# Node tiles on ScalarE's queue, the last panel's own units in its middle, passage steps by engine, the final scaling on two engines

## The chip, the cores and the metric

The kernel runs on one core of one Trainium2 chip. The metric is the device time of one execution in microseconds (us), as the median of several runs.

## The reference

`adj` is an 8192 x 8192 float32 matrix A, `x` is 8192 x 128. Everything is float32. Cut to what matters:

```python
# layer 0
Ap = a * A;  Ap[i, i] += 1 - a;  deg = Ap.sum(axis=1)
x = layernorm(x + relu((Ap @ x) / deg[:, None] @ W.T + b))
# layer 1
xt  = logmap0(x)                                     # row scale by artanh(norm)/norm
par = A   * sigmoid((xt @ wp[:d])[:, None] + (xt @ wp[d:])[None, :] + bp)
chi = A.T * sigmoid((xt @ wc[:d])[:, None] + (xt @ wc[d:])[None, :] + bc)
x = layernorm(x + proj(expmap0(par @ xt + chi @ xt)))
```

## The kernel before, in words

A is cut into blocks of 1024 x 1024, so there are 8 panels of rows. Every load of A is one DMA of 1 MiB (two tiles of 128 rows) and goes into one of 10 buffers, the ring: entries 0 to 6 from the start, 7 to 9 after layer 0. SyncE (SP) issues these loads in the order of the list LOADS, each when its entry is free.

**Layer 0** is a loop over 256 pairs (32 for each panel). TensorE multiplies a pair with two node tiles of x (L1108), and VectorE adds it to the sums for the degrees (L884, L888). The node tiles stand in xA. They come in 16 groups of four DMAs of 64 KiB (L498), and SP issues a group ahead of every second load of the first panel. TensorE waits at pair q for group q // 2. ScalarE's queue begins with nine small DMAs of constants, then loads a panel of x transposed. VectorE waits for the constants at pair 2, before it adds that pair.

After each panel comes its **passage**: some twenty steps on four engines (POOL folds the degree sums, PE sums them and applies W, VectorE and ScalarE normalise and take the log map, PE turns the result and makes the two score vectors). Each step has a tick (T_DEG, T_INV, ... T_COPY), the place in the loop at which every engine that takes part issues it. For the last panel the ticks run beside layer 1: tick t is issued ahead of unit LATE0 + 2t, on every engine alike (LATE0 is 154, the first unit after layer 0).

**Layer 1** has 512 units, one for each pair of panel p and tile jt of 128 rows. A unit is: two sigmoids on ScalarE (L720 chi, L737 par), a product with A's tile on POOL (L537) and one on VectorE (L986), their sum on VectorE (L995), and two matmuls of 512 columns on TensorE, which sum over jt (L1180). In the trace each of these stands as two records. Some units, the list APART, leave out the sum and use two more matmuls instead (L1186). 154 units run in layer 0's loop, the rest after it, panel by panel. Two units share a load of A and one of its transpose. The eight **own units** of a panel, those on the diagonal block, need only A: TensorE turns the tile itself (L1196, turn_own), and for that it waits for all four loads of the diagonal block, whose entries come free after the eighth turn. Own units stand last in each of panels 3 to 7. Units of panel 7 are numbers 448 to 511.

The par scores of a unit stand in a PSUM slot. There are two slots in turn until SLOT_THREE (unit LATE0 + 48), three from there, because the passage uses the other one (E). A fourth chi buffer is used from MORE (unit LATE0 + 30), and APART begins eight units after it.

**Finals.** After the last unit of a panel its sum is taken out (L760), squared (L771), reduced to norms (L1205, then a root, L776), turned (L1215), scaled and added to the residual (L1014), and normalised (L1022 to L793), in steps among the next panel's units. Panel 7's final has no units beside it. Its last steps are the eight pieces of the scaling on ScalarE (L793) and one store of 512 KiB (L486).

Of the kernel before, what the change touches and what calls it, by code (L numbers as in the profile page):

```python
# [11 lines left out]
P = 128  # L12
# [36 lines left out]
T_OWN = 27  # L49

def early_groups():
# [8 lines left out]
def plan():  # L61
# [18 lines left out]
    for p, tiles in order:  # L80
        if len(tiles) == UPP:
            own = range(p * TPP, (p + 1) * TPP)
            tiles = [jt for jt in tiles if jt not in own] + list(own)
        groups.append((p, tiles, NPAN - 1))
        units += [(len(groups) - 1, p, jt) for jt in tiles]
# [54 lines left out]

SLOT_TWO, SLOT_THREE = LATE0, LATE0 + 48

# [112 lines left out]

MORE = LATE0 + 30

# [20 lines left out]
def adj_resnorm_kernel(nc, x_g, xT, g_blk, a_blk, WT, b_row, alpha, w_par, b_par, w_chi, b_chi, out):  # L278
    with ExitStack() as ctx:
# [147 lines left out]
        bias_ready = sem("bias_ready")  # L427
        o_ready = sem("o_ready")
        out_done = sem("out_done")

# [22 lines left out]
        def _(sp):  # L453
# [35 lines left out]
            for kind, j, e, before, _ in LOADS:  # L489
                if kind == "pair":  # L490
                    r, q = divmod(j, PPP)
                    if r == 0 and q % 2 == 0:
                        G = q // 2
                        src = x_g[G].rearrange("(a t) (c s d) -> s a c t d", t=2, s=2, d=D)
                        for h in range(2):
                            for c in range(2):
                                at = G * GC + c * 2 * D
                                sp.dma_start(xA[h * P // 2:(h + 1) * P // 2, at:at + 2 * D]  # L498
                                             .rearrange("a (t d) -> a t d", t=2), src[h, :, c]).then_inc(x_in[G], 16)
                    src = g_blk[q // 4, r, (q % 4) * 2 * P:(q % 4 + 1) * 2 * P, :]  # L500
# [14 lines left out]
            store(NPAN - 2)  # L515
            store(NPAN - 1)
            sp.wait_ge(out_done, 16 * NPAN)

# [94 lines left out]
        def _(act):  # L613
# [174 lines left out]
            def final_normalise(k, i):  # L788
# [4 lines left out]
                ins = act.activation(t, t, ACT.Identity, bias=s_mb[:, j:j + 1], scale=s_rs[:, j:j + 1])  # L793
                if i == TPP - 1:
                    ins.then_inc(o_ready, 1)

            def final(k, step):
# [12 lines left out]
                if k == NPAN - 2:  # L810
                    if step == L_ROOT:
                        final_deviation(k)
                    if L_NORM <= step < L_NORM + TPP:
                        final_normalise(k, step - L_NORM)

            for dst, src in (
                (alph[:, :], alpha.rearrange("(a d) -> a d", a=1).to_broadcast([P, 1])),
# [8 lines left out]
                act.dma_start(dst, src).then_inc(const_in, 16)  # L826
            act.wait_ge(ident_ready, 4)
            load_xT(0)
            scale_xT(0)
# [10 lines left out]
            for n in range(N_EARLY, UNITS):  # L840
                if (n - LATE0) % 2 == 0:
                    passage(NPAN - 1, (n - LATE0) // 2)
                for k, (_, b) in enumerate(FINALS):
# [8 lines left out]
                sigmoids(n)  # L852
            k = NPAN - 1
            evacuate(k)
            square(k)
# [3 lines left out]
            final_deviation(k)  # L859
            for i in range(TPP):  # L860
                final_normalise(k, i)

        @block.vector
        def _(dve):
# [211 lines left out]
            for n in range(N_EARLY, UNITS):  # L1076
                if (n - LATE0) % 2 == 0:
                    passage(NPAN - 1, (n - LATE0) // 2)
                for k, (_, b) in enumerate(FINALS):
                    final(k, n - b)  # L1080
                if n == N_EARLY and PAIRS - 1 in UNIT_AT:
                    key(n - 1)
                first_product(n)
                key(n)
# [6 lines left out]
            variances(k)  # L1091
            final_inverse(k)

        @block.tensor
        def _(pe):
# [135 lines left out]
            for n in range(N_EARLY, UNITS):  # L1231
                if (n - LATE0) % 2 == 0:
                    passage(NPAN - 1, (n - LATE0) // 2)
                for k, (_, b) in enumerate(FINALS):
# [39 lines left out]
```

## Time and profile before

| | us |
|---|---|
| median of three runs (2233.01 to 2239.25) | 2234.77 |
| the profiled execution | 2237.35 |
| its span | 2235.5 |
| TensorE busy | 2039.8 |
| VectorE busy | 1935.9 |
| POOL busy | 1334.1 |
| ScalarE busy | 1326.9 |

The mean granted clock of TensorE is 0.976. Numbers below are from the profiled execution, in us from the start of its span. Layer 0 ends at about 1266, the last load of A is there at 2190.9, and the last matmul of layer 1 ends at 2215.3.

### The profile page before, as it was taken

What the parts mean: (1) busy time and instruction counts of PE and PEld (TensorE: products, weight loads), DVE (VectorE), ACT (ScalarE), POOL (GpSimd) and SP (SyncE); (2) the same over time, 40 slices, a digit from 0 to 9 for tenths busy, and PEclk for the clock granted to TensorE, in tenths of its full rate; (3) what the DMA queues carried; (4) which work ended last, traced back from release to release, by engine and by line L of the source; (5) the groups of instructions that cost most, each with busy time, mean ns of one, the idle gap of its engine ahead of it and who ended that gap; (6) DMA issues with size and microseconds to landing.
All of it is one profiled execution on the core that took longest, in us unless ns stands there. A gap on an engine that the chain in (4) does not pass through costs nothing. (4 is left out here: it accounts for less than half of the span.)

```text
span 2235.5 us, 18654 instructions
## 1 busy us (share of the span) xinstructions
PE 2039.8 (91%) x5240; PEld 919.1 (41%) x5240; DVE 1935.9 (87%) x1854; ACT 1326.9 (59%) x1512; POOL 1334.1 (60%) x607
## 2 busy tenths in 40 slices
PE   8999999999999999999999976998888889889886
PEld 3344444444444434444444432343344334334334
DVE  4676878988989988998998988898998998989996
ACT  0011324454454454453453587889888989999996
POOL 0000305435455555643543676999998998999995
PEclk9999999999999999999999988999999999999998
DMA  9998989899889988888888998999999999998992
GB/s 313 333 343 300 387 299 365 361 366 381 361 347 403 405 344 358 347 357 338 369 356 316 421 421 317 384 363 421 421 393 403 421 420 376 421 421 347 421 421 97
DMA packets 129207, 818.29 MB, mean 366 GB/s; under 512 B 14912, under 2 KB 27456, under 8 KB 33360
## 3 DMA queue, kind: packets, MB, share of 16 engines
q1 hardware_dynamic: 122304, 796.97, 89.1%
q10 hardware_dynamic: 6800, 20.13, 2.5%
q8 instruction: 43, 0.70, 0.1%
q14 instruction: 60, 0.49, 0.1%
HBM read 808.59 MB, written 8.45 MB: 365 GB/s over the span
## 5 line engine op out<-in xcount | busy, mean ns | idle before, releaser
L537 POOL TENSOR_TENSOR chi<-chi,ring 128x1024 f32<-128x1024 f32 x323 | 826.9, 2573 | 662.7 <-ACT chi L720 603.5
L1180 PE MATMUL ps<-keys,xtA 128*128 128x512 f32 x2048 | 986.4, 615 | 135.4 <-DVE keys L995 106.1
L1108 PE MATMUL ps<-ring,xA 128*128 128x512 f32 x2048 | 922.5, 600 | 37.9 <-DMA ring<-in_g_blk 33.6
L737 ACT ACTIVATE ps<-scores,prcr 128x1024 f32<-128x1024 f32 x472 | 521.9, 1106 | 389.5 <-DVE keys L995 379.2
L1180 PEld LDWEIGHTS ps<-keys,xtA 128*128 128x128 f32 x2048 | 382.3, 195 | 668.1 <-issue 629.0
L888 DVE TENSOR_TENSOR dsum<-dsum,ring 128x2048 f32<-128x2048 f32 x240 | 593.2, 2472 | 44.7 <-DMA ring<-in_g_blk 37.4
L1108 PEld LDWEIGHTS ps<-ring,xA 128*128 128x128 f32 x2048 | 386.5, 192 | 533.3 <-issue 468.8
L995 DVE TENSOR_TENSOR keys<-ps,chi 128x1024 f32<-128x1024 f32 x395 | 483.7, 1224 | 78.2 <-issue 29.2
L986 DVE TENSOR_TENSOR ps<-ps,ring 128x1024 f32<-128x1024 f32 x381 | 465.9, 1223 | 74.2 <-ACT ps L737 71.1
L720 ACT ACTIVATE chi<-scores,prcr 128x1024 f32<-128x1024 f32 x430 | 488.7, 1137 | 61.0 <-PE ps L1186 45.8
L537 POOL TENSOR_TENSOR chi<-chi,xA 128x1024 f32<-128x1024 f32 x107 | 251.9, 2372 | 32.4 <-ACT chi L720 32.3
L537 POOL TENSOR_TENSOR xA<-xA,ring 128x1024 f32<-128x1024 f32 x49 | 116.2, 2372 | 1.6 <-ACT xA L720 1.6
L995 DVE TENSOR_TENSOR keys<-ps,xA 128x1024 f32<-128x1024 f32 x82 | 100.4, 1225 | 6.6 <-DVE ps L986 2.4
L986 DVE TENSOR_TENSOR ps<-ps,xA 128x1024 f32<-128x1024 f32 x76 | 93.0, 1224 | 14.4 <-ACT ps L737 12.9
L530 POOL TENSOR_TENSOR dsum<-dsum 128x1024 f32<-128x1024 f32 x8 | 18.8, 2354 | 139.6 <-DVE dsum L888 137.2
L720 ACT ACTIVATE xA<-scores,prcr 128x1024 f32<-128x1024 f32 x82 | 93.0, 1134 | 0.4 <-ACT yb L671 0.4
L630 ACT ACTIVATE small<-mv,epsc 128x8 f32<-128x8 f32 x8 | 2.4, 301 | 150.6 <-DVE mv L922 150.6
L537 POOL TENSOR_TENSOR xA<-xA 128x1024 f32<-128x1024 f32 x33 | 78.3, 2374 | 5.0 <-ACT xA L720 5.0
L1186 PE MATMUL ps<-chi,xtA 128*128 128x512 f32 x140 | 65.8, 592 | 0.0
L884 DVE TENSOR_TENSOR dsum<-ring 128x1024 f32<-128x1024 f32 x16 | 34.3, 2182 | 31.8 <-PE ps L1117 17.4
L546 POOL TENSOR_TENSOR acc<-taken,acc 128x1024 f32<-128x1024 f32 x15 | 37.4, 2490 | 31.0 <-ACT taken L753 31.0
L720 ACT ACT_TABLE_LOAD x28 | 35.9, 1283 | 26.8 <-DVE prcr L954 22.6
(109 smaller groups left out, 818.6 us busy)
## 6 DMA issues: line engine op xcount, KB each, us to landing
ring<-in_g_blk SPq DMA_DIRECT2D x461, 1024.0 KB, 10.0
ring<-in_a_cols SPq DMA_DIRECT2D x186, 1024.0 KB, 9.9
xA<-in_a_cols SPq DMA_DIRECT2D x70, 1024.0 KB, 10.9
xA<-in_g_blk SPq DMA_DIRECT2D x31, 1024.0 KB, 12.6
scores<-plcl_d ACTq DMA_DIRECT2D x22, 512.0 KB, 8.1
xA<-in_x_g SPq DMA_DIRECT2D x64, 64.0 KB, 13.4
yb<-in_xT ACTq DMA_DIRECT2D x8, 512.0 KB, 8.8
x_d<-res ACTq DMA_DIRECT2D x8, 512.0 KB, 8.5
```

Of the source, the lines that this page charges most:

```text
L530: pool.tensor_tensor(out=dsum[:, 0:BP], in0=dsum[:, 0:BP], in1=dsum[:, BP:2 * BP], op=ALU.add).then_inc(folded, 1)
L537: pool.tensor_tensor(out=chi(n), in0=chi(n), in1=half(t, n), op=ALU.mult).then_inc(m2_ready, 1)
L546: pool.tensor_tensor(out=at, in0=taken[:, :], in1=at, op=ALU.add).then_inc(acc_added, 1)
L720: act.activation(chi(n), scores[:, row, 1, :], ACT.Sigmoid, bias=prcr[:, 2 * jt + 1:2 * jt + 2]).then_inc(c_ready, 1)
L737: act.activation(dst, scores[:, row, 0, :], ACT.Sigmoid, bias=prcr[:, 2 * jt:2 * jt + 1]).then_inc(p_ready, 1)
L884: dve.tensor_tensor(out=half(dsum, h), in0=half(t0, h), in1=half(t, h), op=ALU.add) \
L888: dve.tensor_tensor(out=dsum[:, :], in0=dsum[:, :], in1=t, op=ALU.add).then_inc(deg_added, 1)
L986: dve.tensor_tensor(out=keys(n) if n in APART else s, in0=s, in1=other, op=ALU.mult).then_inc(m1_ready, 1)
L995: dve.tensor_tensor(out=keys(n), in0=slots[SLOT_OF_UNIT[n][0]], in1=chi(n), op=ALU.add).then_inc(k_ready, 1)
L1108: ins = pe.matmul(Y[:, h * BANK:(h + 1) * BANK], xA[:, tile * D:(tile + 1) * D], t[:, tt * BP + h * BANK:tt * BP + (h + 1) * BANK], start= ...
L1180: ins = pe.matmul(outp[:, h * BANK:(h + 1) * BANK], xtA[:, jt * D:(jt + 1) * D], keys(n)[:, h * BANK:(h + 1) * BANK], start=begins, stop=i ...
L1186: ins = pe.matmul(outp[:, h * BANK:(h + 1) * BANK], xtA[:, jt * D:(jt + 1) * D], chi(n)[:, h * BANK:(h + 1) * BANK], start=False, stop=is_ ...
```

## The change

The node tiles are issued by ScalarE: groups 0 and 1, then the constants, then groups 2 to 15, then the first panel of x transposed. The own units of panel 7 stand after its first 24 units. The last passage has a table of places for each engine in place of the common ticks; these are single units and begin and end earlier. SLOT_THREE and MORE are earlier. At the end ScalarE loads the table with the square root before it takes out the last panel, and the scaling of the last panel is split, four pieces on ScalarE and four on VectorE, with a store for each half.

```diff
+LATE_PE = {2: T_DEG, 6: T_LIN, 27: T_TURN, 31: T_PRP, 34: T_ROWS}
+LATE_ACT = {14: T_STD, 17: T_X1, 19: T_SQ, 21: T_NRM, 24: T_LN, 27: T_XT, 32: T_XTT, 39: T_COPY}
+LATE_DVE = {5: T_INV, 10: T_RES, 11: T_STATS, 14: T_RSTD, 21: T_LOGA, 24: T_FAC, 34: T_PRCR}
...
             own = range(p * TPP, (p + 1) * TPP)
-            tiles = [jt for jt in tiles if jt not in own] + list(own)
+            rest = [jt for jt in tiles if jt not in own]
+            tiles = rest + list(own) if p < NPAN - 1 else rest[:24] + list(own) + rest[24:]
...
-SLOT_TWO, SLOT_THREE = LATE0, LATE0 + 48
+SLOT_TWO, SLOT_THREE = LATE0, LATE0 + 41
...
-MORE = LATE0 + 30
+MORE = LATE0 + 16
... (SyncE)
-                    if r == 0 and q % 2 == 0:
-                        G = q // 2
-                        src = x_g[G].rearrange("(a t) (c s d) -> s a c t d", t=2, s=2, d=D)
-                        for h in range(2):
-                            for c in range(2):
-                                at = G * GC + c * 2 * D
-                                sp.dma_start(...).then_inc(x_in[G], 16)
...
-            store(NPAN - 1)
-            sp.wait_ge(out_done, 16 * NPAN)
+            half_panel = TPP // 2 * P
+            for h, there, count in ((0, o_ready, NPAN), (1, o_half, 1)):
+                at = (NPAN - 1) * BP + h * half_panel
+                sp.wait_ge(there, count)
+                sp.dma_start(out[at:at + half_panel, :]..., x1f[...]...).then_inc(out_done, 16)
+            sp.wait_ge(out_done, 16 * (NPAN + 1))
... (ScalarE)
-                if i == TPP - 1:
+                if i == (TPP - 1 if k < NPAN - 1 else TPP // 2 - 1):
                     ins.then_inc(o_ready, 1)
...
+            def load_nodes(G):
+                src = x_g[G].rearrange("(a t) (c s d) -> s a c t d", t=2, s=2, d=D)
+                for c in range(2):
+                    for h in range(2):
+                        at = G * GC + c * 2 * D
+                        act.dma_start(xA[h * P // 2:(h + 1) * P // 2, at:at + 2 * D]
+                                      .rearrange("a (t d) -> a t d", t=2), src[h, :, c]).then_inc(x_in[G], 16)
+            load_nodes(0)
+            load_nodes(1)
             for dst, src in (...):                      # nine constants
                 act.dma_start(dst, src).then_inc(const_in, 16)
             act.wait_ge(ident_ready, 4)
+            for G in range(2, NG):
+                load_nodes(G)
             load_xT(0)
             scale_xT(0)
...
-                if (n - LATE0) % 2 == 0:
-                    passage(NPAN - 1, (n - LATE0) // 2)
+                passage(NPAN - 1, LATE_ACT.get(n - LATE0))     # LATE_DVE, LATE_PE on VectorE, TensorE
...
             k = NPAN - 1
+            act.preload_act_table(ACT.Sqrt)
             evacuate(k)
...
-            for i in range(TPP):
+            for i in range(TPP // 2):
                 final_normalise(k, i)
... (VectorE, after final_inverse)
+            dve.wait_ge(bias_ready, k + 1)
+            for i in range(TPP // 2, TPP):
+                t, j = x1f[k % 2][:, i * D:(i + 1) * D], k * TPP + i
+                ins = dve.tensor_scalar(t, t, s_rs[:, j:j + 1], s_mb[:, j:j + 1], ALU.mult, ALU.add)
+            ins.then_inc(o_half, 1)
```

## Rows read from the trace of the kernel before

**Rows 1.** The page: what all DMA moved, in 40 slices.

```profile
GB/s 313 333 343 300 387 299 365 361 366 381 361 347 403 405 344 358 347 357 338 369 356 316 421 421 317 384 363 421 421 393 403 421 420 376 421 421 347 421 421 97
```

**Rows 2.** Windows: start:end, length, engines' busy us, granted clock, DMA share, GB/s.

```profile
20.00:110.00 90.00, 88.98 (x203) 36.74 (x202) 58.41 (x26) 0.72 (x1) 0.00 (x0) 1.00 1.05 338
130.00:1260.00 1130.00, 1095.14 (x2799) 498.76 (x2798) 991.86 (x862) 476.34 (x623) 469.41 (x171) 0.99 0.90 356
1266.60:1350.00 83.40, 63.16 (x140) 26.66 (x138) 71.18 (x83) 67.97 (x84) 67.84 (x30) 0.86 1.02 421
1350.00:1440.00 90.00, 69.98 (x153) 29.57 (x154) 75.77 (x74) 70.74 (x74) 69.07 (x30) 0.87 0.86 333
2060.00:2190.00 130.00, 112.84 (x267) 45.39 (x265) 119.67 (x126) 122.41 (x131) 122.87 (x62) 1.00 1.01 421
```

**Rows 3.** ScalarE's waits, 1340 to 1440: us in total, times, longest.

```profile
ACT yb L667 <- PE ps L1132: 6.7, 1, 6.7
...
ACT xtA L661 <- DVE small L950: 3.0, 1, 3.0
ACT yb L671 <- PE ps L1144: 2.6, 1, 2.6
```

**Rows 4.** Windows of 10 us, panel 6's own units.

```profile
2040.00:2050.00 10.00, 10.00 (x48) 6.58 (x47) 9.86 (x9) 9.38 (x10) 10.00 (x5) 1.00 0.18 76
2050.00:2060.00 10.00, 8.89 (x22) 3.75 (x21) 9.64 (x10) 8.68 (x9) 8.67 (x4) 1.00 0.88 353
```

**Rows 5.** Timeline of SP, 2028 to 2055: start, us, what is issued.

```profile
2032.17 0.33 SPq L513 DMA_DIRECT2D ring<-in_g_blk  x1
2050.14 0.33 SPq L513 DMA_DIRECT2D ring<-in_a_cols  x1
```

**Rows 6.** Timeline, last own units and the last final.

```profile
2187.25 1.95 PE L1180 MATMUL ps<-keys,xtA 128*128 128x512 f32 x4 [0.20 <-DVE keys L995]
...
2190.94 0.50 PE L1196 MATMUL ps<-ident,xA 128*128 128x128 f32 x2 [1.03 <-DMA xA<-in_a_cols]
...
2209.94 5.32 PE L1180 MATMUL ps<-keys,xtA 128*128 128x512 f32 x12
...
2211.41 1.22 DVE L995 TENSOR_TENSOR keys<-ps,chi 128x1024 f32<-128x1024 f32 x1
...
2217.42 1.28 ACT L776 ACT_TABLE_LOAD   x1
...
2219.69 0.18 ACT L776 ACTIVATE fs<-ps 128x8 f32<-128x8 f32 x1 [0.99 <-PE ps L1205]
...
2223.24 2.16 DVE L1014 SCALAR_TENSOR_TENSOR res<-ps,fs,res 128x128 f32<-128x128 f32 x8 [0.66 <-POOL fs L569]
...
2228.96 3.19 ACT L793 ACTIVATE res<-res,fs 128x128 f32<-128x128 f32 x8 [0.87 <-POOL fs L576]
2232.17 0.39 SPq L486 DMA_DIRECT2D out<-res  x1
```

**Rows 7.** Timeline, the first 30 us.

```profile
0.72 2.60 SPq L498 DMA_DIRECT2D xA<-in_x_g  x4
...
3.36 1.07 SPq L513 DMA_DIRECT2D ring<-in_g_blk  x2
...
10.79 49.62 PE L1108 MATMUL ps<-ring,xA 128*128 128x512 f32 x110 [10.79 <-DMA ring<-in_g_blk]
...
19.64 2.29 DVE L888 TENSOR_TENSOR dsum<-dsum,ring 128x2048 f32<-128x2048 f32 x1 [2.06 <-issue]
...
26.45 2.29 DVE L888 TENSOR_TENSOR dsum<-dsum,ring 128x2048 f32<-128x2048 f32 x1 [1.30 <-DMA ring<-in_g_blk]
```

**Rows 8.** DMA queues, 7 to 12 us: q1 is SP's, q10 ScalarE's.

```profile
q1 hardware_dynamic: 246, 1.88, 91.1%
q10 hardware_dynamic: 282, 0.00, 3.0%
```

**Rows 9.** All DMA packets, 20 to 110 us.

```profile
DMA packets 11200, 30.44 MB, mean 338 GB/s; under 512 B 1246, under 2 KB 7902, under 8 KB 7902
```

More of the change, by code:

```diff
@@ L428, in adj_resnorm_kernel @@
         o_ready = sem("o_ready")
+        o_half = sem("o_half")
         out_done = sem("out_done")
@@ L491, in _ @@
                     r, q = divmod(j, PPP)
-                    if r == 0 and q % 2 == 0:
-                        G = q // 2
-                        src = x_g[G].rearrange("(a t) (c s d) -> s a c t d", t=2, s=2, d=D)
-                        for h in range(2):
-                            for c in range(2):
-                                at = G * GC + c * 2 * D
-                                sp.dma_start(xA[h * P // 2:(h + 1) * P // 2, at:at + 2 * D]
-                                             .rearrange("a (t d) -> a t d", t=2), src[h, :, c]).then_inc(x_in[G], 16)
                     src = g_blk[q // 4, r, (q % 4) * 2 * P:(q % 4 + 1) * 2 * P, :]
@@ L515, in _ @@
             store(NPAN - 2)
-            store(NPAN - 1)
-            sp.wait_ge(out_done, 16 * NPAN)
+            half_panel = TPP // 2 * P
+            for h, there, count in ((0, o_ready, NPAN), (1, o_half, 1)):
+                at = (NPAN - 1) * BP + h * half_panel
+                sp.wait_ge(there, count)
+                sp.dma_start(out[at:at + half_panel, :].rearrange("(c p t) d -> p c (t d)", p=P, t=2),
+                             x1f[(NPAN - 1) % 2][:, h * half_panel:(h + 1) * half_panel]
+                             .rearrange("p (c e) -> p c e", e=2 * D)).then_inc(out_done, 16)
+            sp.wait_ge(out_done, 16 * (NPAN + 1))
         @block.gpsimd
@@ L1076, in _ @@
             for n in range(N_EARLY, UNITS):
-                if (n - LATE0) % 2 == 0:
-                    passage(NPAN - 1, (n - LATE0) // 2)
+                passage(NPAN - 1, LATE_DVE.get(n - LATE0))
                 for k, (_, b) in enumerate(FINALS):
@@ L1231, in _ @@
             for n in range(N_EARLY, UNITS):
-                if (n - LATE0) % 2 == 0:
-                    passage(NPAN - 1, (n - LATE0) // 2)
+                passage(NPAN - 1, LATE_PE.get(n - LATE0))
                 for k, (_, b) in enumerate(FINALS):
```

## The prediction

> **What bounds the kernel now.** I read the page's GB/s row first, then windows by stage, then waits and timelines where the change touches. The GB/s row [rows 1] shows slices at 420 or 421 and nothing above: I take 421 as what this kernel's loads of 8 KB packets can reach. The windows [rows 2] then give three regimes. In the first panel TensorE is busy 88.98 of 90 us and the DMA engines too (share 1.05, only 338 GB/s). In the rest of layer 0 TensorE is busy 1095 of 1130 us, so it is the bound, and any delay at the start is carried to the end. After layer 0 the DMA engines move 421 GB/s (1266.6 to 1350, 2060 to 2190), except in three places: 1350 to 1440 (333 GB/s), the own units of each panel, and the end, where nothing is loaded after 2190.9. What moves no bytes away can gain there by taking away idle time of the DMA engines, and only that.
>
> **The last passage.** Idle DMA in 1350 to 1440 is (421 - 333) / 421 x 90 = 18.8 us [rows 2]. Its cause is in the waits of ScalarE [rows 3]: step XTT (L667) waits 6.7 us for TensorE's turn, XT (L661) 3.0 for VectorE, COPY (L671) 2.6 for TensorE: 12.3 us together. All follow one pattern. ScalarE runs ahead of VectorE and TensorE in units, and a step that needs another engine's step at the same unit, or two units before, makes it wait until that engine has caught up; then VectorE has no sigmoids. The new tables widen these distances: TURN to XTT from 0 to 5 units, ROWS to COPY from 2 to 5, LOGA to LN and FAC to XT from 2 to 3. They also move LOGA from unit 26 to 21, FAC from 30 to 24, so VectorE's work for these two falls into the stretch that is bound by DMA anyway (there VectorE is busy 71.2 of 83.4 us). No distance gets shorter: DEG to INV goes from 2 to 3, LIN to RES stays 4. An earlier MORE makes units 178 and 186 APART as well: two additions of 1.22 us less on VectorE, four matmul halves more on TensorE, which is busy 70 of 90 us and hides them; the third slot seven units earlier only loosens a wait. Ends: nothing, if VectorE is the bound there (75.8 busy of 90), and -18.8, if all idle DMA goes. The value nearest to the row of waits, with some of the 2-to-3 distances not fully cured: **-12 us**.
>
> **Own units in the middle of panel 7.** Now all four diagonal loads must be there before the first turn is complete (2190.9), and eight own units follow at TensorE's pace, until 2209.94 + 5.32 = 2215.3 [rows 6]: 24.4 us without a load. After the change the last loads serve an ordinary pair of units. Behind the last landing stand four VectorE operations (two units' product and sum, 1.22 each by L995 [rows 6]), a handover and one unit of TensorE: 4 x 1.22 + 0.1 + 1.95 = 7.0 us. That is 17.4 less. But the middle gets the idle that own units make elsewhere. SP issues nothing between 2032.17 and 2050.14 [rows 5], as the next entry comes free with the eighth turn, and the DMA engines lose (0.82 + 0.12) x 10 = 9.4 us [rows 4]. No score rows are loaded in panel 7's middle to fill it, as none are there. Net 9.4 - 17.4 = **-8 us**. Ends: -17.4 (no new idle) and +0.5 (the whole 17.9 us of SP's pause lost).
>
> **The end.** Eight scalings take 3.19 us [rows 6], four 1.6. VectorE's four, by its L1014 at 2.16 / 8 = 0.27 each, take 1.1 and lie beside them. Then SP issues two stores one behind the other, the second 0.4 later than a single one would be: 1.6 - 0.4 = **-1.2 us** (ends 0 and -2). The early table load gains nothing: the old one runs from 2217.42 to 2218.70, and the root waits for TensorE's norms until 2219.69 anyway. If it were to force a reload for the copy, it would cost 1.28.
>
> **The start.** This one costs. SP's first load of A is issued at 0.72 instead of 3.36 [rows 7], so TensorE may start up to 2.6 us earlier than 10.79. But the two queues now compete. A group of node tiles, 256 KiB, is 512 packets of 512 bytes (packets under 2 KB but not under 512 B [rows 9]), a load of A only 128 of 8 KB. So beside a full SP queue a group takes 10 us, and TensorE needs one each 6.9. Followed through: about 400 packets of groups 0 and 1 pass before A's loads flow (at about 4 us), the other 620 need 12.5, so pair 2 can start at about 18, where VectorE's part of it starts at 19.64 now. Behind them come nine constants with 128 packets each, 1152. SP's queue holds 9 MiB by then (seven entries and the two that come free before VectorE blocks on the constants at pair 2), 1152 packets, of which 650 to 700 are gone. So some 475 constants' packets take turns for 9.5 us; then SP's queue is dry and the rest runs alone. Alone, a small packet takes 3.9 ns: 3298 packets of 8 KB are 27.0 MB, 64 us at 421 GB/s, and the other 26 us hold 6656 [rows 9]. That is 2.6 us for the rest and 2 for group 2, one more for the landing: pair 4 starts at about 33. Now its VectorE part starts at 26.45 [rows 7], and TensorE, which keeps pace from 10.79, has it then too. From there groups come in time, since TensorE's pace leaves SP's queue dry for part of each pair, and with TensorE busy 88.98 of 90 nothing is caught up: **+6 us**. Ends: -2.6 (no contention felt) and +17 (all 1152 in turn, 23 us). VectorE's delay at pair 2 is hidden by its 2.29 us a pair against 3.4 of TensorE. The panel of x transposed now comes last in ScalarE's queue, about when panel 0 is done; if it were later, it would add to this.
>
> On this step the row showed turns by packet. The Trainium skill (DMA: Bandwidth & Descriptors, "Issuing engines are not separate DMA queues") says that DMAs of all issuing engines run on the same 16 DMA engines and interleave, and that issuing from several saves only the sequencer's time. This trace agrees with the first half. By the second half alone the sum would have -2.6 here in place of +6, and end near 2211.
>
> **Sum.** -12 - 8 - 1.2 + 6 = -15.2. Against the profiled execution's own 2237.35 that is 2222; this execution lies 2.6 above the median of the runs (2234.77), and against that it is **2219.5**.
>
> **Rivals.**
> - Node tiles cost nothing or gain (chance 0.13). For it: SP's issue of four takes 2.6 us ahead of the first load, and DMA is work-conserving. Against it: rows 8. Time: 2219.5 - 8.6 = 2211.
> - VectorE takes over (0.13). For it: it is busy 119.7 of 130 us in the last panel and 75.8 of 90 in the passage, so both stretches may give back little: -4 and -3. Against: idle time sits behind named waits. Time: 2234.8 - 4 - 3 - 1.2 + 6 = 2232.5.
> - Node tiles starve TensorE for the whole first panel (0.08), the slower side. If SP's queue never runs dry, each group takes 512 / 50 = 10.2 us instead of 6.9, over 14 groups +47 us, with the stall at the constants +53; less 21 that is slower by 32: 2267. It decides at whether seven ring entries land while TensorE waits; they need 18 us at 50 packets per us, so I think that it does run dry.
> - The forecast (0.66), its own range 2211 to 2228.
>
> **Range and chances.** 2207 to 2233 takes in the first rival, and the second just. What counts as a difference is 0.3% (6.7 us). Faster than 2228: the forecast, the first rival and a little of the second, 0.81. Within 0.3%: most of the second, 0.11. Slower: 0.08.
>
> **What would show it.** First panel: TensorE's second group of pairs waits for a DMA of xA, with pair 4 near 33, and the constants' users (oma, L1056) at 30 instead of 16.7; wrong if pair 4 starts before 27. Passage: L667's and L671's waits gone, DMA over 380 GB/s between unit 180 and 208. Own units: a window near 0.2 DMA share in the middle of panel 7, and 7 us from the last landing to the last matmul. End: L793 four times, 1.6 us, two stores. The prediction is wrong if 1350 to 1440 keeps its idle DMA with the waits gone, or if layer 0 doesn't carry the delay of the start.

## The result, and the profile after

The changed kernel takes 2230.4 us (median of 14 runs, 2225.04 to 2234.28), the kernel before 2234.6 (median of 14, 2228.63 to 2241.34). The ratio is 0.9978, with an interval of 0.9967 to 0.9988. So the change is worth some 5 us, and I had forecast 15. The time lies in my range and the sign is right; the size is a third, closer to the rival in which VectorE takes over (2232.5) than to the forecast (2219.5). The profiled execution took 2234.23 us with a span of 2232.4 us; the one before had a span of 2235.5.

The windows first, in the stretches of [rows 2] and some of 10 us. Columns: stretch, length, busy time of TensorE, its weight load, VectorE, ScalarE and GpSimd with instruction counts, granted clock, DMA share, GB/s.

```profile
20.00:110.00 90.00, 88.03 (x205) 38.60 (x204) 67.43 (x39) 3.71 (x3) 0.00 (x0) 1.00 1.01 351
130.00:1260.00 1130.00, 1091.91 (x2785) 497.70 (x2786) 985.66 (x860) 472.67 (x620) 467.10 (x170) 0.99 0.89 353
1266.60:1350.00 83.40, 62.89 (x145) 27.68 (x143) 71.21 (x86) 64.03 (x81) 64.24 (x28) 0.86 1.01 419
1350.00:1440.00 90.00, 75.07 (x174) 31.44 (x175) 84.17 (x74) 77.41 (x81) 76.72 (x34) 0.92 0.90 360
2060.00:2190.00 130.00, 116.45 (x320) 52.01 (x319) 120.22 (x127) 122.34 (x130) 122.68 (x62) 1.00 0.95 391
2120.00:2130.00 10.00, 10.00 (x48) 6.58 (x47) 9.86 (x19) 8.25 (x9) 9.07 (x5) 1.00 0.42 174
2130.00:2140.00 10.00, 9.11 (x26) 3.75 (x24) 9.86 (x9) 9.94 (x11) 7.52 (x4) 1.00 0.72 280
2190.00:2200.00 10.00, 8.47 (x18) 3.28 (x19) 9.41 (x9) 10.00 (x11) 10.00 (x5) 1.00 1.01 414
```

Against [rows 2] the passage (1350 to 1440) moves 360 GB/s where it moved 333: of 18.8 us of idle DMA, (421 - 360) / 421 x 90 = 13 are left. VectorE went from 75.8 to 84.17 busy of 90, and that is the row to see (its count includes time in which an operation is held up, see below). The own units leave their hole in the middle now (2120 to 2140: share 0.42 and 0.72), and loads run at 414 until 2200, where nothing was loaded after 2190.9 [rows 6]. In 2120 to 2140 VectorE is busy 9.86 of 10 twice, and TensorE 10.00 and 9.11; GpSimd has some idle time (9.07 and 7.52), but VectorE does not wait in that hole.

The start, TensorE and then the first user of the small constants (start, duration, group; in brackets idle before and what ended it), against [rows 7]:

```profile
14.83 8.77 PE L1129 MATMUL ps<-ring,xA 128*128 128x512 f32 x16 [14.83 <-DMA xA<-in_x_g]
23.90 7.11 PE L1129 MATMUL ps<-ring,xA 128*128 128x512 f32 x16 [0.30 <-DMA xA<-in_x_g]
32.68 7.53 PE L1129 MATMUL ps<-ring,xA 128*128 128x512 f32 x17 [1.67 <-DMA xA<-in_x_g]
```
```profile
25.95 0.15 DVE L1072 TENSOR_SCALAR oma<-alph 128x1 f32<-128x1 f32 x1 [14.65 <-DMA wr<-in_w_chi]
```

Pair 4 starts at 32.68, where I had 33; pair 2 at 23.90 instead of my 18; pair 0 at 14.83, where I had allowed 10.8 or earlier. The constants' first user starts at 25.95, where I had 30.

Where the time goes is read best from a few marks in every kernel of the same work: the start of TensorE's first matmul of a pair of layer 0, the start of ScalarE's sigmoid of a unit of layer 1, and the end of the last matmul of a unit (us, read from each trace's instructions; "unit 154" is the first one late).

```
                 pair 4  pair 32  pair 255 | unit 154  unit 202  unit 232  unit 511 | last unit  span
before             26.6    128.3    1262.9 |   1264.3    1422.3    1491.2    2204.5 |   2215.3  2235.5
before, again      26.3    124.0    1263.3 |   1264.6    1422.6    1491.4    2204.5 |   2215.3  2235.5
after              32.7    130.5    1269.9 |   1270.5    1420.3    1491.6    2205.0 |   2213.1  2232.4
b_nodes_act        31.4    129.1    1265.5 |   1265.9    1424.9    1493.8    2206.8 |   2217.6  2237.9
u1_nodes_on_sp     27.1    124.9    1260.8 |   1262.4    1411.1    1481.7    2195.1 |   2203.3  2222.1
u2_old_passage     32.0    129.7    1265.8 |   1267.4    1425.4    1494.3    2208.0 |   2216.1  2235.7
u3_own_last        31.7    129.4    1265.6 |   1266.5    1416.1    1487.5    2200.1 |   2210.9  2229.4
p_fewer_bytes      32.1    129.8    1265.6 |   1265.9    1415.9    1486.6    2198.3 |   2206.5  2226.6
v1_x1_at_18        26.7    124.5    1260.2 |   1261.5    1407.1    1477.8    2191.8 |   2200.0  2219.4
v2_wider           26.9    124.6    1260.8 |   1262.2    1406.4    1478.2    2192.3 |   2200.4  2219.9
p_fewer_early      26.3    124.0    1266.5 |   1267.9    1416.7    1487.0    2199.9 |   2208.1  2226.6
c_act_2k           30.1    129.6    1265.1 |   1266.1    1415.3    1486.5    2199.7 |   2207.8  2227.0
v3_sp_2k           23.9    121.6    1257.3 |   1258.5    1404.3    1475.4    2188.7 |   2196.8  2216.0
p_half_pool        26.3    126.7    1262.7 |   1263.9    1409.7    1480.5    2194.7 |   2202.2  2221.2
```

Two things keep one from reading too much into one pair of traces. Both traces of the kernel before end alike, yet differ by 4 us at pair 32. And "after" alone is at 1269.9 at pair 255, while four kernels with the same start are at 1265.5 to 1265.8; this one execution lost 4 us in layer 0 that its kind does not lose. With node tiles on SP (512-byte packets) pair 255 starts anywhere from 1260.2 to 1266.5 in seven traces, so a difference of 2 or 3 us at that mark in one pair of traces lies within that spread.

### The profile page after: what moved, and what is told of

It is laid out like the page before. It is cut to its first block, busy times and chain, and to the rows that moved or that the text cites. A ratio compares the mean times of both kernels' runs of the same rounds, so it can differ in the third digit from the quotient of the medians.

```text
span 2232.4 us, 18671 instructions
## 1 busy us (share of the span) xinstructions
PE 2035.9 (91%) x5248; PEld 921.2 (41%) x5248; DVE 1938.1 (87%) x1856; ACT 1324.6 (59%) x1508; POOL 1334.0 (60%) x607
## 3 DMA queue, kind: packets, MB, share of 16 engines
HBM read 808.59 MB, written 8.45 MB: 366 GB/s over the span
## 4 chain that ended last, share of the span: by engine, by line
PE 44%; POOL 17%; issue 11%; DVE 11%; ACT 10%; DMA 5%; ACTq 1%; DVEq 0%; POOLq 0%; SPq 0%
PE ps L1129 28%; POOL chi L541 13%; PE ps L1201 11%; DVE dsum L904 3%; ACT chi L724 3%; DMA ring<-in_g_blk 3%; DVE ps L1002 3%; POOL xA L541 3%; ACT ps L741 2%; DMA ring<-in_a_cols 2%; PE ps L1217 1%; DVE keys L1011 1%; POOL acc L550 1%; ACT L724 1%; ACT xA L724 1%
## 5 line engine op out<-in xcount | busy, mean ns | idle before, releaser
L904 DVE TENSOR_TENSOR dsum<-dsum,ring 128x2048 f32<-128x2048 f32 x240 | 592.1, 2467 | 23.6 <-DMA ring<-in_g_blk 16.9
L1011 DVE TENSOR_TENSOR keys<-ps,chi 128x1024 f32<-128x1024 f32 x426 | 521.6, 1224 | 81.7 <-issue 28.4
L724 ACT ACTIVATE chi<-scores,prcr 128x1024 f32<-128x1024 f32 x426 | 483.8, 1136 | 16.1 <-DMA scores<-plcl_d 8.9
L541 POOL TENSOR_TENSOR chi<-chi,xA 128x1024 f32<-128x1024 f32 x105 | 247.3, 2376 | 26.2 <-ACT chi L724 26.2
L541 POOL TENSOR_TENSOR xA<-xA,ring 128x1024 f32<-128x1024 f32 x53 | 126.0, 2378 | 13.1 <-ACT xA L724 13.1
L724 ACT ACTIVATE xA<-scores,prcr 128x1024 f32<-128x1024 f32 x86 | 98.0, 1140 | 43.2 <-PE ps L1207 43.0
L534 POOL TENSOR_TENSOR dsum<-dsum 128x1024 f32<-128x1024 f32 x8 | 18.8, 2352 | 127.0 <-DVE dsum L904 124.8
L1207 PE MATMUL ps<-xA,xtA 128*128 128x512 f32 x148 | 70.2, 597 | 0.0
L1011 DVE TENSOR_TENSOR keys<-ps,xA 128x1024 f32<-128x1024 f32 x49 | 60.0, 1225 | 3.1 <-POOL xA L541 1.3
```

The source lines that it names most:

```text
L541: pool.tensor_tensor(out=chi(n), in0=chi(n), in1=half(t, n), op=ALU.mult).then_inc(m2_ready, 1)
L724: act.activation(chi(n), scores[:, row, 1, :], ACT.Sigmoid, bias=prcr[:, 2 * jt + 1:2 * jt + 2]).then_inc(c_ready, 1)
L904: dve.tensor_tensor(out=dsum[:, :], in0=dsum[:, :], in1=t, op=ALU.add).then_inc(deg_added, 1)
L1011: dve.tensor_tensor(out=keys(n), in0=slots[SLOT_OF_UNIT[n][0]], in1=chi(n), op=ALU.add).then_inc(k_ready, 1)
L1207: ins = pe.matmul(outp[:, h * BANK:(h + 1) * BANK], xtA[:, jt * D:(jt + 1) * D], chi(n)[:, h * BANK:(h + 1) * BANK], start=False, stop=is_ ...
```

## The experiments

**Each part undone.** My theory was the prediction's: start +6, passage -12, own units -8. The rival: the passage and the own units give little, since VectorE and the engines around it bind and the loads do not.

*u1_nodes_on_sp*: the changed kernel with its node tiles back in SP's queue.

```
@@ SP's loads
+    if r == 0 and q % 2 == 0:      # four DMAs of x_g[G], as before
@@ ScalarE
-    load_nodes(0)
-    load_nodes(1)
...
-    for G in range(2, NG):
-        load_nodes(G)
```

> The changed kernel with the node tiles back on SyncE's queue, all else kept. Theory A (the two queues take turns packet by packet, and what the first panel loses is carried by TensorE to the end): pair 4 of the first panel starts near 26.5 us instead of 32.7, pair 32 near 128.3 instead of 130.5, unit 0 about 2.2 us earlier; the further 3.5 to 5 us that the changed kernel lags by the end of layer 0 are not made by the queue, so unit 154 comes 2 to 3 us earlier, and the kernel is faster by 2 to 3 us (ratio to before near 0.997). Rival (the whole 7 us lag at unit 154 comes from the queue): unit 154 7 us earlier, total faster by 5 to 7 us. Second rival (the lag is taken up after layer 0, since the loads' pace there decides): units from 202 on at the same places as in the changed kernel, total unchanged within 1 us.

Measured: 2223.97 us, ratio to before 0.9958 (0.9945 to 0.9971). Pair 4 is back at 27.1 and pair 32 at 124.9; TensorE runs from 11.01 without a stop. By the ratios the start costs the change 4.5 us (0.9978 less 0.9958), more than the 2 to 3 of my theory here and just under the rival's 5 to 7, and the rest of the change is worth more than the total shows.

*u2_old_passage*: the changed kernel with the old rule for the last passage, MORE and the third slot.

```
-SLOT_TWO, SLOT_THREE = LATE0, LATE0 + 41
+SLOT_TWO, SLOT_THREE = LATE0, LATE0 + 48
-MORE = LATE0 + 16
+MORE = LATE0 + 30
-passage(NPAN - 1, LATE_ACT.get(n - LATE0))      # and _DVE, _PE
+if (n - LATE0) % 2 == 0:
+    passage(NPAN - 1, (n - LATE0) // 2)
```

> The changed kernel with the last passage at its old common ticks and SLOT_THREE and MORE at their old places. Theory A (the steps by engine take away 7 to 8 us): unit 202 and all later ones come about 7 to 8 us later than in the changed kernel, so 1431 instead of 1423.5, and the total is 2237 to 2238 us (ratio to before 1.001 to 1.002). Rival (the late position at unit 154 is caught up in any case, and the new tables give nothing or cost): unit 202 at 1424 to 1426, total near 2230. DMA idle from 1350 to 1440 near 19 us by A, as before.

Measured: 2237.51 us, ratio 1.0016 (1.0005 to 1.0027). GpSimd's product of unit 154 to that of unit 202 takes 156.3 us in it and in the kernel before, 149.5 in after, 148.4 in u1, 149.3 in u3. The new tables are worth 7 us, not 12.

*u3_own_last*: the changed kernel with panel 7's own units last.

```
-tiles = rest + list(own) if p < NPAN - 1 else rest[:24] + list(own) + rest[24:]
+tiles = rest + list(own)
```

> The changed kernel with panel 7's own units last again. Theory A (idle DMA engines at own units are a full ring, not lost time; the end is bound by POOL at 2.33 us a unit): POOL's product of unit 511 starts at the same time within 1 us, the last load lands 10 us earlier (2191), and the last matmul ends 2.0 to 2.5 us later (2215.3 to 2215.7), for own units trail POOL by TensorE's 2.67 a unit; total slower by 2 us. Rival (my prediction: DMA bound, 17.4 less at the end and 9.4 back in the middle): total slower by 8 us.

Measured: 2231.21 us, ratio 0.9984 (0.9975 to 0.9994). Its interval and that of the change overlap; -8 us would be 0.0036. The marks split it: from the last unit's product on GpSimd to its last matmul 8.6 us here and 6.1 in after, but 712.6 us before and 713.7 after from unit 232's product to unit 511's. Net -1.4 us. The 1.1 us of it are small: eight kernels with the own units in the middle and nothing else changed behind unit 232 lie between 712.3 and 714.9, four with them last between 712.4 and 713.2.

**Do the loads bind at all?** *p_fewer_bytes* is the changed kernel with half of each transposed load of A from unit 232 on left out (the other half keeps what lay there).

```
+if kind == "trn" and 2 * j >= 232:
+    half_of = entry(e).rearrange("p (t c) -> p t c", t=2)[:, :, 0:BP // 2]
+    sp.dma_start(half_of, <the same rows, columns 0:BP // 2>)
```

> The changed kernel, but from unit 232 on each load of the transpose brings only the left half of each of its rows (25% fewer bytes for an ordinary pair); the products take the rest from what the entry held. Theory A (after about unit 200 the kernel is bound by POOL, VectorE and their couplings and the ring is ahead of them, although the DMA engines are busy all the time): units 232 to 511 keep their pace, 715 us, total unchanged within 3 us, DMA share near 0.8. Rival (the prediction's reading: 421 GB/s is the bound there): a panel of 72 units falls from 185 us towards POOL's 2.33 us a unit, 168 to 175, total faster by 25 to 60 us.

Measured: 2229.43 us, ratio 0.9976 (0.9964 to 0.9989), against the change's 0.9978. The windows of 1520 to 1650 and 2060 to 2190:

```profile
1520.00:1650.00 130.00, 113.45 (x268) 47.31 (x267) 120.42 (x140) 114.75 (x119) 122.19 (x65) 0.98 0.89 322
2060.00:2190.00 130.00, 115.39 (x307) 50.28 (x306) 120.74 (x127) 122.55 (x130) 123.10 (x63) 1.00 0.84 306
```

With 306 GB/s in place of 391 the three engines are as busy as in after's row of the same stretch, and unit 232 to unit 511 takes 711.4 us (by GpSimd's products) instead of 713.7; the lowest of the eight kernels with all bytes is 712.3. More than a fifth of the bytes gone is worth 2 us at most. This refutes the base of my prediction for layer 1.

*p_fewer_early* asks the same of the last passage. It is u1 without those halves of the loads for units 154 to 231.

```
+if kind == "trn" and LATE0 <= 2 * j < 232:
+    <the same half load>
```

> The changed kernel with the node tiles on SyncE's queue, but from unit 154 to 231 each load of the transpose brings only the left half of its rows; the products take the rest from what the entry held. It asks what binds units 154 to 202 with 421 GB/s moved. Theory A (here the loads do bind, since ScalarE and VectorE wait with the ring empty: 8.1 us for each entry): unit 202 5 to 12 us earlier than 1414.3. Rival (the passage's steps and the copies bind here too, as POOL and VectorE do later): unit 202 within 2 us. After 202 the same pace by both.

Measured in one run: 2228.47 us. It arrived late at unit 154 (1267.9, u1 1262.4), from layer 0, which the edit does not touch. From product 154 to 202 it takes 148.6 us, u1 148.4.

```profile
1266.60:1350.00 83.40, 60.47 (x137) 26.64 (x135) 72.01 (x86) 64.98 (x81) 65.28 (x29) 0.83 0.85 321
1350.00:1440.00 90.00, 77.81 (x180) 32.20 (x180) 84.34 (x75) 79.62 (x83) 76.93 (x34) 0.93 0.82 286
```

My theory here, that the loads do bind this stretch and unit 202 comes 5 to 12 us earlier, was wrong. Even the stretch that showed share 1.01 and 419 GB/s in after (1.00 and 408 in u1) has the same pace at 321 GB/s. A full DMA share was the mark of a ring filled ahead, not of a bound.

**The start alone.** *b_nodes_act*: the kernel before, with only the node tiles moved to ScalarE's queue, as the change has them.

```
@@ before.py, SP
-    <four DMAs of x_g[G] at every second pair of r == 0>
@@ ScalarE
+load_nodes(0)
+load_nodes(1)
 <the nine constants>
+for G in range(2, NG):
+    load_nodes(G)
```

> The kernel before with only the node tiles moved to ScalarE's queue, in the change's order. Theory A (turns by packet; the loss stays): pair 0 starts at 15 to 16 us, pair 4 at 32, pair 32 at 129.5 to 130.5, and the kernel is 2 to 5 us slower than before (ratio 1.001 to 1.002). Rival (DMA work is conserved and the groups come early, so that the first panel ends as before): pair 32 within 1 us of the kernel before, total the same.

Measured: 2240.67 us against 2235.69, ratio 1.0023 (1.0013 to 1.0033), +5 us. Pair 32 at 129.1, against 124.0 in b_again (below).

*c_act_2k*: the changed kernel, with each node group as one DMA of 128 packets of 2 KB instead of four with 512 of 512 bytes, the array laid out for it in advance.

```
-for c in range(2):
-    for h in range(2):
-        act.dma_start(<quarter of the group, 512 B runs>)
+act.dma_start(xA[:, G * GC:(G + 1) * GC], x_g[G]).then_inc(x_in[G], 16)
```

> The changed kernel with node groups laid out so that each is one DMA of 128 packets of 2 KB in place of 512 packets of 512 bytes, still on ScalarE's queue. Theory A (two queues take turns packet by packet, whatever the sizes): a group needs only as many turns as a load of A, so pair 0 starts at 8 to 10 us instead of 14.8, pair 2 no later than 17, pair 4 waits less or not at all (the constants' 1152 packets still stand ahead of group 2: up to 27 to 29 us instead of 32.7), pair 32 at 119 to 124 instead of 130. Rival (it is bytes that are shared, or start-up latency of ScalarE's queue): pair 0 stays at 13 to 15.5 us. Total by A: ratio to before 0.994 to 0.996.

Measured: 2228.79 us, ratio 0.9968 (0.9956 to 0.9980). TensorE's first 40 us:

```profile
6.38 15.61 PE L1124 MATMUL ps<-ring,xA 128*128 128x512 f32 x32 [6.38 <-DMA xA<-in_x_g]
30.06 10.13 PE L1124 MATMUL ps<-ring,xA 128*128 128x512 f32 x19 [8.08 <-DMA xA<-in_x_g]
```

The same bytes in a quarter of the packets let pair 0 start at 6.38 instead of 14.83. Then TensorE waits 8.08 us for group 2, which stands behind the constants: 1152 packets of 4 bytes and more, unchanged. Part of the 8.45 us is issue time: ScalarE's queue takes 5.51 us to issue after's first eight DMAs, 0.89 for the two here, so some 2.3 us less for group 0 (an estimate from these two). The rest is the turn by packet, and the counts of the two queues show it: in after 619 packets of SP's queue and 620 of ScalarE's pass from 8 to 20 us, and here 1026 and 1022 from 8 to 28, nearly all of the constants among them. For the length of the wait it is packets that count, not bytes. My theory had pair 32 at 119 to 124 and a ratio of 0.994 to 0.996, and missed both. The early gain is lost behind the constants: pair 4 starts at 30.1, where the kernels of the other layout have 31.4 to 32.7. But no packet of SP's queue passes from 30 to 36 us, as SP issued no load of A between 15.2 and 33.0, and pair 32 is at 129.6, as in the other kernels with this queue.

*v3_sp_2k*: v1 (below) with the 2 KB packets, in SP's queue.

```
-<four DMAs of x_g[G] in SP's queue>
+sp.dma_start(xA[:, G * GC:(G + 1) * GC], x_g[G]).then_inc(x_in[G], 16)
```

> The kernel with node tiles on SyncE's queue and X1 at unit 18, with the same 2 KB packets. Theory A (in the first panel the 512-byte packets also cost DMA time, 3.9 ns each; TensorE is near its own pace of 3.43 us a pair anyway): SP's issue ahead of the first load falls from 2.6 to 0.6 us, so pair 0 at 8.7 to 9 instead of 10.7, pair 32 at 119.5 to 122 instead of 124.5, total 2 to 4 us faster than with 512-byte packets (2221.7), near 2218. Rival (the first load's landing has a fixed start-up): pair 0 at 10 or later and total unchanged.

Measured: 2218.88 us, ratio 0.9924 (0.9910 to 0.9938): pair 0 at 7.9, no stop after it, 3 us less than v1 up to the end (their intervals overlap a little). It is the fastest kernel here.

*b_again*: the kernel before, unchanged, once more.

> The kernel before once more, for one more trace of it. Theory A (its first trace had a slow first panel by chance, 128.3 us for pair 32, where four kernels with the same first panel have 124.0 to 124.9): pair 32 at 124 to 125.5, total again 2229 to 2241. Rival (something in the change makes the first panel faster with node tiles on SyncE's queue): 128 again.

Measured in one run: 2237.3 us; pair 32 at 124.0, and at 1263.3 for pair 255 like the first. So the reference for the first panel is 124, not the 128.3 of the first trace, and the node tiles' cost at pair 32 is 5 us.

**What is left in the passage.** In after, TensorE waits once for 7.33 us, where the kernel before waits 3.37 at the same place. ScalarE's side of it and TensorE's:

```profile
1327.88 3.17 ACT L639 ACTIVATE res<-res,small 128x128 f32<-128x128 f32 x8
1331.52 1.02 ACT L757 ACTIVATE taken<-ps 128x1024 f32<-128x1024 f32 x1 [0.46 <-ACT res L639]
```
```profile
1332.59 8.68 PE L1201 MATMUL ps<-keys,xtA 128*128 128x512 f32 x16 [7.33 <-ACT taken L757]
```

The new table puts step X1 (unit 17 of the passage) ahead of the copy that frees PSUM, at the same unit. *v1_x1_at_18* is u1 with that step one unit later:

```
-LATE_ACT = {14: T_STD, 17: T_X1, 19: T_SQ, ...
+LATE_ACT = {14: T_STD, 18: T_X1, 19: T_SQ, ...
```

> The changed kernel with the node tiles on SyncE's queue and step X1 at unit 18 instead of 17. At 17 it stands ahead of the copy that takes out a group's sum at the same unit (171), and TensorE waited 7.3 us for that copy. Theory A (the tables lose 11 us up to unit 181 partly through this collision): TensorE's wait falls to 3 to 4 us, unit 181 comes 2 to 4 us earlier than with X1 at 17 (1364.0), unit 202 0 to 3 us earlier (1414.3). Rival (the lag at 181 is a loan that the ring gives back anyway): unit 181 earlier, unit 202 and the total unchanged within 0.5 us.

Measured: 2221.69 us, ratio 0.9939 (0.9926 to 0.9953). The wait is 3.79 us:

```profile
1319.21 8.69 PE L1205 MATMUL ps<-keys,xtA 128*128 128x512 f32 x16 [3.79 <-ACT taken L765]
```

154 to 202 takes 145.3 us, 3.1 less than u1. The intervals of the two totals overlap a little, but the marks keep the gain: v1 is 4.0 us ahead of u1 at unit 202 and 3.3 at unit 511. Something else moved with it, though: VectorE's series LOGA takes 1.2 us in v1 and 5.2 in u1 (why, see below). So the 3 us belong to the edit, and are not shown to be the shorter wait alone.

*v2_wider* is v1 with the late steps further apart:

```
-LATE_PE  ... 27: T_TURN, 31: T_PRP, 34: T_ROWS
+LATE_PE  ... 29: T_TURN, 33: T_PRP, 36: T_ROWS
-LATE_ACT ... 27: T_XT, 32: T_XTT, 39: T_COPY
+LATE_ACT ... 29: T_XT, 34: T_XTT, 41: T_COPY
-LATE_DVE ... 24: T_FAC, 34: T_PRCR      SLOT_THREE = LATE0 + 41
+LATE_DVE ... 27: T_FAC, 36: T_PRCR      SLOT_THREE = LATE0 + 43
```

> As the one with X1 at 18, and FAC at unit 27 instead of 24, with XT at 29, TURN at 29, PRP 33, XTT 34, PRCR and ROWS 36, COPY 41, SLOT_THREE two units later. Theory A (LOGA and FAC at units 21 and 24 hold VectorE for 5.4 and 7.8 us within three units, with two slots ScalarE then waits for it): FAC takes 4 to 6 us, unit 181 at 1355 to 1360, unit 202 1 to 3 us earlier than with FAC at 24. Rival (loads decide between 154 and 200): unit 202 within 1 us.

Measured: 2221.85 us, ratio 0.9940 (0.9927 to 0.9953): nothing. FAC took 4.8 us instead of 8.2, as expected. Unit 181 came 6 us earlier and unit 202 0.9; the marks of unit 232 and 511 are back at v1's.

**Which engine binds the last panels.** *p_half_pool* is v1 in which GpSimd multiplies only the left half of each tile from unit 232 on (the right half stays unmultiplied). If GpSimd were the bound, the panels would go faster; by the rival VectorE and ScalarE are.

```
+w = slice(0, BP // 2 if n >= 232 else BP)
-pool.tensor_tensor(out=chi(n), in0=chi(n), in1=half(t, n),
+pool.tensor_tensor(out=chi(n)[:, w], in0=chi(n)[:, w], in1=half(t, n)[:, w],
```

> The kernel with node tiles on SyncE's queue and X1 at unit 18, but from unit 232 on POOL multiplies only the left half of each chi tile (the right half goes on without A). It asks what binds layer 1 once loads are shown not to. Theory A (POOL's 2.33 us a unit is the pace of most units, and with it gone the next are the loads at 421 GB/s, 68 MiB or 169 us a panel plus 4 MB of score rows and residuals): a panel of 72 units falls from 185 us to 176 to 180. Rival (VectorE's two operations of 1.22 us, or the waits of the finals on ScalarE, bind): a panel stays within 2 us of 185.

Measured in one run: 2223.02 us, v1's time within its spread. The stretch 2060 to 2190, first in v1 and then in this kernel, and this kernel's waits of GpSimd after 2000 (for whom: us, times, longest):

```profile
2060.00:2190.00 130.00, 115.94 (x306) 50.68 (x307) 122.28 (x129) 120.63 (x127) 125.74 (x63) 1.00 0.93 383
2060.00:2190.00 130.00, 118.37 (x322) 52.99 (x322) 125.45 (x131) 126.05 (x134) 71.45 (x65) 1.00 0.96 400
```
```profile
POOL chi L550 <- ACT chi L733: 65.6, 56, 3.9
POOL xA L550 <- ACT xA L733: 24.5, 19, 3.8
```

GpSimd falls from 125.74 busy us to 71.45 and now waits for ScalarE. From unit 232's product to unit 511's it takes 713.3 us, and v1 713.8. But this is a sum of two differences. The three stretches of 72 units take 185.8, 186.7 and 187.5 us instead of v1's 184.6, 185.2 and 186.1: GpSimd does not bind there. The 63 steps of panel 7 take 153.3 instead of 157.8: there its multiplications did hold the pace, by 4.5 us (157.4 to 157.8 in the six other kernels looked at).

VectorE needs a product and a sum per unit, 1.26 and 1.14 from start to start, 2.4 us a unit, whatever the others do. Panel 7 without half of GpSimd's work runs at 2.43 us a unit, close to that. The stretches of 72 units take 2.58 to 2.60 a unit, finals and own units included. Over units 232 to 511 VectorE is busy 656 of v1's 714 us, ScalarE 647 and GpSimd 663. Which of them, or which handover between them, sets the pace there is not shown by a run; that it is not the loads, nor GpSimd alone, is.

## Why the prediction was right or wrong

**What bounds layer 1: wrong, and this is the step that failed.** "After layer 0 the DMA engines move 421 GB/s", and so "what moves no bytes away can gain there by taking away idle time of the DMA engines, and only that". The row was read rightly, the conclusion was not tested. SP issues a load as soon as an entry of the ring is free. In the last panel of after that is 15 to 24 us before GpSimd's product uses it, and the load lands 7 us or more before that use, so the DMA engines look full at whatever pace the units have. p_fewer_bytes and p_fewer_early show that 21 to 24 per cent fewer bytes per us leave the pace as it was. In [rows 2] the three engines at 119.7, 122.4 and 122.9 of 130 were the better clue, and my rival "VectorE takes over" came nearest, at 0.13; worked out with its terms (-4, -3, -1.2, +6) it is off by 2 us of the total, though part of that is luck, as its terms for the passage and the own units miss by 3 and 1.6 in opposite directions.

**The last passage: predicted -12, measured -7.** The waits of [rows 3] are gone, as predicted. But in all ScalarE waits 12.5 us in this stretch, where it waited 19.1: the wait for VectorE came back at other places. ScalarE's largest left between 1340 and 1440 (whom it waited for: us, times, longest):

```profile
ACT ps L741 <- DVE keys L1002: 4.6, 1, 4.6
ACT xA L724 <- PE ps L1207: 4.4, 4, 2.3
ACT ps L741 <- DVE keys L1011: 3.1, 1, 3.1
```

And my test for "wrong" was met: 1350 to 1440 keeps 13 of its 18.8 us of idle DMA with the waits gone. The term that was mis-sized is this one: I priced the passage by ScalarE's named waits (12.3 us), and what VectorE and the other engines let it gain was 7. X1 ahead of the take-out copy took some of the gain (v1 gives back 3 us). And two series of VectorE three units apart grew:

```profile
1347.60 2.10 DVE L953 SCALAR_TENSOR_TENSOR small<-small 128x8 f32<-128x8 f32 x1
1349.73 2.27 DVE L954 TENSOR_SCALAR small<-small 128x8 f32<-128x8 f32 x1
...
1359.51 0.17 DVE L960 TENSOR_TENSOR small<-small 128x8 f32<-128x8 f32 x1
...
1359.95 2.11 DVE L962 TENSOR_TENSOR small<-small 128x8 f32<-128x8 f32 x1
1362.09 2.27 DVE L963 TENSOR_TENSOR small<-small 128x8 f32<-128x8 f32 x1
1364.40 2.26 DVE L964 SCALAR_TENSOR_TENSOR small<-small 128x8 f32<-128x8 f32 x1
```

An operation on 8 columns takes 0.17 us or 2.1 to 2.3. Start to end the two series take 5.3 and 8.0 us here and 4.2 each before (there 2.26 and 1.05 in one, 2.28 and 0.36 in the other, are the only long ones). My plan had them cost the same wherever they stand. The trace says what made them long. GpSimd beside the second series:

```profile
1359.67 2.36 POOL L541 TENSOR_TENSOR xA<-xA,ring 128x1024 f32<-128x1024 f32 x1 [5.39 <-ACT xA L724]
1361.99 2.35 POOL L541 TENSOR_TENSOR chi<-chi,ring 128x1024 f32<-128x1024 f32 x1
1364.29 2.35 POOL L541 TENSOR_TENSOR chi<-chi,xA 128x1024 f32<-128x1024 f32 x1
```

L960 runs while GpSimd is idle and takes 0.17. L962, L963 and L964 each start during a multiplication and end 0.02 to 0.03 us after it; L966 is short again, with GpSimd idle. All long operations of these series end so, in every trace looked at: before, after, u1, v1 and v2. A reciprocal of the same shape (L961) takes 0.20 beside a multiplication, so not every operation is held up. The Trainium skill (SBUF — State Buffer, "Who interferes with whom") says that VectorE and GpSimd share a port pair under an exclusive lock that is held for a whole instruction. The ends of the long operations agree. How much of the total the longer series cost is open: v2 shortened them by 3.4 us against v1, and the total stayed.

"No distance gets shorter" was a misreading of my own tables: STD to RSTD, NRM to LOGA and LN to FAC go from 2 units to 0, and XT to TURN from 4 to 0. In these VectorE or TensorE follows ScalarE, and after's trace shows no wait for ScalarE at these steps between 1266 and 1440.

**Own units in the middle: predicted -8, measured -1.4.** The hole in the middle came (8.6 us of idle DMA in 2120 to 2140, where I had 9.4), and loads run to 2200. The way from the last landing (2200.2) to the last matmul's end (2213.1) is 12.9 us, not 7: the last load lands well before it is used. The tail was shortened by 2.5 us, not 17.4, because hardly anything had been waiting for loads there (TensorE's turn, 1.03 us in [rows 6]); for the same reason the hole cost about 1 and not 9.4. The steps that failed are thus both terms, as both took idle DMA for lost time.

**The end: predicted -1.2, measured about -1.**

```profile
2215.34 2.76 PE L1226 MATMUL ps<-ones,dsum 128*128 128x1 f32 x16 [2.20 <-ACT dsum L775]
2227.41 1.65 ACT L797 ACTIVATE res<-res,fs 128x128 f32<-128x128 f32 x4 [0.88 <-POOL fs L580]
```
```profile
2227.41 1.11 DVE L1112 TENSOR_SCALAR res<-res,fs 128x128 f32<-128x128 f32 x4 [0.64 <-POOL fs L580]
```
```profile
2229.09 0.90 SPq L518 DMA_DIRECT2D out<-res  x2
```

Four scalings of 1.65 beside four of 1.11, and the two stores right behind: against [rows 6] 1.54 us less for the scaling. From the last matmul of a unit to the first store it is 16.0 us instead of 16.9, so 0.6 went elsewhere; TensorE's norms took 2.76 instead of 2.20, in a stretch where the granted clock was 0.82 (2210 to 2220; before 0.96). The second store did not lengthen the end: from the first store's issue to the end of the span it is 3.3 us in both. The early table load ran in idle time and gained nothing, as predicted.

**The start: predicted +6, measured +5.** The mechanism held, turns by packet, and with it the choice of the row [rows 8] over the notion that issuing from several queues is free. The Trainium skill (DMA: Bandwidth & Descriptors, "Queues, rings and completion order") says that each DMA engine takes turns between its queues by packet. After's trace agrees, counted in the profile's packets (packets, MB, share), from 8 to 20 us:

```profile
q1 hardware_dynamic: 619, 4.43, 94.1%
q10 hardware_dynamic: 620, 0.28, 9.4%
```

and from 22 to 24 us, with SP's queue nearly dry:

```profile
q10 hardware_dynamic: 1221, 0.21, 66.9%
q1 hardware_dynamic: 42, 0.21, 30.8%
```

My steps in it were worse than their sum, and that pair 4 came at 32.68 for my 33 is luck, two errors that cancel. I let some 400 packets of groups 0 and 1 pass before A's loads flow; none passed in the first 4 us, while 80 packets of A's loads did. So nearly all of the two groups took turns, and the last of their eight DMAs landed at 23.8 us (pair 2 at 23.9 for my 18). I let 475 of the constants' packets take turns for 9.5 us; but SP's queue was nearly dry by then, and the nine constants landed from 24.0 to 25.9. And I gave group 2 some 3 us behind them; beside two new loads of A its four DMAs landed from 28.0 to 32.5. Layer 0 carried the delay: at pair 255 the traces have 4 to 5 us between u1, v1 and v2 and the kernels with the moved node tiles, 2.3 between the kernel before and b_nodes_act. Alone, in b_nodes_act, it costs 5 us by the times; its one traced execution ends only 2.4 later than the kernel before.

**The sum.** +5 - 7 - 1.4 - 1 = -4.4, against -4.9 (0.9978 of 2234.6) measured.

**Open.** Why the execution of after, and that of p_fewer_early, lost 4 to 6 us more in layer 0 than others of their start. What v2's 6 us at unit 181 are lost to by unit 202. And what sets the pace of the panels before the last, where neither the loads nor GpSimd alone do.

## What to carry to other kernels

A DMA share of 1.0 shows that the queue is full, not that anyone waits for it: look for compute that waits for a landing, or take bytes away, before pricing idle DMA. When waits of an engine that runs ahead are taken away, the gain is no more than what the engines behind it can go faster, so add up that engine's operations per unit first (2.4 us of VectorE here), and expect part of the wait to come back elsewhere (19.1 us became 12.5). Small packets in a second queue get the same turns as large ones, so moving loads to an idle issuer can delay them by their packet count; make the packets larger first.

## What the runs showed of the hardware that I had not expected

- VectorE's operations on 128x8 tiles took 0.17 us or 2.1 to 2.3 us, in the same series, and the long ones ended 0.02 to 0.03 us after the GpSimd multiplication of 2.35 us beside which they had started.
- Each 256 KiB of node tiles as one DMA of 128 packets of 2 KB, instead of four with 512 of 512 bytes, let TensorE start at 6.38 instead of 14.83 us beside a full second queue, and at 7.9 instead of 10.7 in one queue.
- From 2060 to 2190 us the DMA engines moved 391 GB/s in one kernel and 306 in another, at the same pace of the engines.
